# Pair weights applied at the copy out of PSUM, and the last layernorm stage handed out again among the engines

## Chip, cores and metric

One core of a Trainium2 chip runs the kernel. The metric is the device time of one execution in microseconds (us). TensorE is named PE in the profile, VectorE DVE, ScalarE ACT, GpSimd POOL and SyncE SP; PEld is PE's loading of weights.

## The reference

For x of 8 batches x 512 tokens x 128 channels (all f32):

```
x = x + layernorm(attn(layernorm(x)))          # a decaying scan between two 128x128 products
h = layernorm(x)
logits = h @ gate                              # 8 experts
w, e = top_k(logits, 2);  w = softmax(w)
out_k = (silu(h @ w0[e_k]) * (h @ w1[e_k])) @ wo[e_k]      # 128 -> 512 -> 128, k = 0, 1
x = x + layernorm(w_0 * out_0 + w_1 * out_1)
```

The softmax over two logits depends on their gap only: with gap = second logit - first logit and t = tanh(gap / 2), the first weight is 0.5 - 0.5 t and the second 0.5 + 0.5 t.

## The kernel before

**Attention part.** It works batch by batch (four tiles of 128 tokens each) and ends, per batch, with the normalised rows `row` (128 channels, then a column with the token's number and a column with its first expert), the two chosen experts, and for each (token, choice) a place in the DRAM tensor `expert_rows`, where every expert has a region. POOL writes them there with 8 indirect DMAs a batch (`send_row`, L394). `top` (L808 to L820) also keeps the gap of the two best logits in `logit_gap`.

**Expert part.** There are 71 tiles (`TILES`) of up to 128 rows of one expert. The code of every engine runs through the same `slots()`: slot t holds x transposed for tile t, the two first layers of tile t-1, the transposing of the gated values of t-2, the last layer of t-3 and the copying out and sending of t-4. SP loads each tile's rows (`load_tile`, L312) into a ring `taken_rows` of 16. ACT does `first_part` (L570, x rounded to x_hi), `take_y` (L587, the last layer's result from PSUM to `y_rows`, a plain copy), `gate_curve` (L575, silu) and `gated_turned` (L580). DVE does `rest_part` (L1099, x_lo), `times_gate_curve` (L1106) and, once in four tiles (`PAIRS`), `pairs_of_tiles` (L1118, L1122), which finds for four tiles whether a row is its token's second choice (`not_first`) and where its result goes (`y_pair`). POOL sends a tile's y with one indirect DMA to `pair_rows` (`send_y`, L405). While batches remain, each phase of 8 slots also carries parts of the attention work (`a_slot`), between the tiles' own instructions; the first 48 tiles (`FULL_TILES`) lie in such phases. `OLD_TILES` is 63: from there on tiles hold only rows of the last batch.

**Last stage.** `pair_rows` holds 2 x 128 values for each token. SP waits until the y of the first 63 tiles has landed and reads batches back in five groups (`GROUPS`: batch 0; 1 and 2; 3 and 4; 5 and 6; 7), the last group after all 71 (L343). A group then goes through:

- DVE `sum_pairs` (L1146): out_0 + r * out_1 with r = w_1 / w_0, one scalar_tensor_tensor per tile of tokens;
- DVE `stats_of` (L1154) and `aggregate` (L1160), then `scaled` (L1165), the variance times w_0 squared;
- POOL `one_over_sd`: plus eps (L438), to the power -0.5 (L442);
- DVE `scale` (L1171), times w_0, and `offset` (L1176);
- ACT `normalise4` (L593), one activation per tile of tokens;
- POOL (L465), in the last group DVE (L1284), adds the result to x; SP writes x to `out` (L351).

`weights` makes w_0, w_0 squared and r once, in slot 61, from ACT's tanh of all gaps (L643, slot 59). The order on DVE is written out by a loop over groups (L1268): sums and statistics of group g stand before scale and offset of group g-1. Group 0's sum lies in slot 69, its statistics in slot 70, its `one_over_sd` on POOL in slot 71, and its `normalise4` on ACT in slot 73, ahead of the last tile's `take_y` in slot 74. After the slots POOL does, for g = 0 to 3, `one_over_sd(g + 1)` and then group g's add, one instruction per group.

Of the kernel before, what the change touches and what calls it, by code (L numbers as in the profile page):

```python
# [14 lines left out]
P = 128  # L15
# [7 lines left out]
ROW = D + 2  # L23
# [27 lines left out]
W_SPLITS = 8  # L51
GROUPS = ((0, 1), (1, 3), (3, 5), (5, 7), (7, 8))


def sandwich_kernel(nc, x_in, w_in_in, b_in_in, w_out_in, b_out_in, decay_in, mix_in,
                    gate_in, w0_in, w1_in, wo_in, out):
    ctx = ExitStack()
    with ctx:
# [70 lines left out]
        logit_gap = sb("logit_gap", [P, B * G])  # L129
        weight = sb("weight", [P, K, B * G])  # L130
        denom = sb("denom", [P, B * G])
        half1 = sb("half1", [P, B * G])
        weight0_square = sb("weight0_square", [P, B * G])
# [25 lines left out]
        not_first = sb("not_first", [P, PAIRS])  # L159
        y_pair = pair("y_pair", [P, PAIRS], I32)  # L160
# [18 lines left out]
        def pair_tile(n, k):  # L179
            at = (n % G * K + k) * D  # L180
            return pairs_in[n // G][:, at:at + D]
# [3 lines left out]
        scaled_var, sd4, inv4, rs4, nm4 = (sb(n, [P, B * G]) for n in (  # L185
            "scaled_var", "sd4", "inv4", "rs4", "nm4"))
# [14 lines left out]
        def before_in(bank_of, b):  # L201
# [13 lines left out]
                   "xn2T_ps xn2T gate_ps gap top8 choice choice_f onehot taken total "  # L215
# [7 lines left out]
        names_c = "xeT_ps x_hi x_lo l1_ps l2_ps silu gated gatedT_ps gatedT y_ps y not_first y_pair"  # L223
# [4 lines left out]
        names_d = "out_end m stats mv scaled sd inv rs nm normed out x1"  # L228
        d = {n: sem("d_" + n) for n in names_d.split()}
        s_exp, s_weight = sem("exp"), sem("weight")  # L230
# [31 lines left out]
        def sums(n):  # L262
            return pair_tile(n, 0)

        def normed_of(first, end):

            return pairs_of(first, end).rearrange("p (n k d) -> p n k d", k=K, d=D)[:, :, 0, :]
# [15 lines left out]
        def _(sp):  # L283
# [73 lines left out]
        def _(pool):  # L357
# [78 lines left out]
            def one_over_sd(g, first, end):  # L436
                pool.wait_ge(d["scaled"], g + 1)
                pool.tensor_tensor(  # L438
                    sd4[:, first * G:end * G], scaled_var[:, first * G:end * G],
# [3 lines left out]
                    inv4[:, first * G:end * G], sd4[:, first * G:end * G],  # L443
                    minus_half[:].broadcast_to([P, (end - first) * G]),
                    ALU.pow).then_inc(d["inv"], 1)
# [16 lines left out]
            for g, (first, end) in enumerate(GROUPS[:-1]):  # L462
# [6 lines left out]
        def _(act):  # L469
# [168 lines left out]
            for k, s, t in slots():  # L638
# [6 lines left out]
                elif t == TILES + 2:  # L645
                    normalise4(0, *GROUPS[0])
# [846 lines left out]
```

## Time and profile before

| | us |
|---|---|
| median of 3 runs | 347.58 (345.55 to 349.6) |
| the profiled execution | 350.95 |
| its span, first to last instruction | 349.2 |
| mean granted TensorE clock | 0.858 of 2.4 GHz |

Busy shares of the span: PE 75%, DVE 57%, POOL 52%, ACT 51%. All rows are of the profiled execution, whose own time is 1.75 us above its span. Times of rows are counted from the span's start. The duration in a row is that of the instruction or the merged group; "[idle before <-releaser]" is the time its engine had stood idle and what ended it.

### The profile page before, as it was taken

Reading aid. Unit: us, or ns where it says so; the run is one execution under the profiler, and the core shown is the slowest. Engines: PE = TensorE matmul, PEld = TensorE weight load, DVE = VectorE, ACT = ScalarE, POOL = GpSimd, SP = SyncE. Lnnn points to the kernel's source line nnn. Section 1 sums busy time; section 2 is a strip of 40 time slices with the busy share of each in tenths; the row PEclk is TensorE's granted clock in tenths of the full one; section 3 lists DMA queues with packets and bytes.
Section 4 is the critical chain, followed back from the end, with each engine's and each line's share of the span. In section 5 each row is a group of like instructions: output and inputs, shape, how many; then the busy total and the mean of one; then the engine's idle time right before and its main releaser. Section 6 shows DMA issues by size and latency. Waiting matters only on the chain.

```text
span 349.2 us, 6768 instructions
## 1 busy us (share of the span) xinstructions
PE 262.5 (75%) x1615; PEld 220.8 (63%) x1615; DVE 199.7 (57%) x896; ACT 179.4 (51%) x436; POOL 180.1 (52%) x199
## 2 busy tenths in 40 slices
PE   1645515579997999699969969969999999995000
PEld 0323513468785888588858858848888888885000
DVE  4787969564662495348347625633334455459763
ACT  3475635345654566354545544524655565554362
POOL 6065567155465656545754764465333333335673
PEclk9975555589999899789989998998999999999555
DMA  6999111211221131013112211331233100190225
GB/s 160 225 362 281 41 38 55 52 33 41 60 57 46 41 76 48 30 52 81 41 35 64 57 47 42 83 92 55 69 85 79 42 23 23 31 401 29 90 60 150
DMA packets 27971, 29.48 MB, mean 84 GB/s; under 512 B 4538, under 2 KB 21148, under 8 KB 27936
## 3 DMA queue, kind: packets, MB, share of 16 engines
q1 hardware_dynamic: 22672, 20.00, 20.2%
q0 software_dynamic: 4544, 8.93, 8.0%
q8 instruction: 16, 0.26, 0.3%
q10 hardware_dynamic: 720, 0.13, 0.2%
q14 instruction: 19, 0.16, 0.2%
HBM read 17.49 MB, written 12.01 MB: 84 GB/s over the span
## 4 chain that ended last, share of the span: by engine, by line
PE 60%; DVE 15%; ACT 8%; another core or an unknown queue 6%; POOL 4%; issue 4%; DMA 2%; SPq 0%; ACTq 0%; DVEq 0%; POOLq 0%
PE bank L1432 14%; PE bank L1381 9%; PE bank L1383 9%; PE bank L1382 8%; PE bank L1416 8%; PE bank L1376 3%; POOL expert_rows L394 2%; PE bank L1317 2%; PE bank L1333 2%; ACT sb_w_raw L593 2%; DVE sb_rs L1171 2%; PE bank L1326 2%; ACT sb_row L524 1%; PE bank L1306 1%
## 5 line engine op out<-in xcount | busy, mean ns | idle before, releaser
L405 POOL DMA_INDIRECT pair_rows<-sb_y_rows,sb_y_pair x71 | 70.4, 991 | 99.3 <-ACT sb_y_rows L587 75.2
L394 POOL DMA_INDIRECT expert_rows<-sb_row,sb_place x64 | 65.1, 1016 | 32.0 <-issue 18.0
L1106 DVE TENSOR_TENSOR sb_w_raw<-bank,sb_w_raw 128x512 f32<-128x512 f32 x71 | 49.0, 690 | 51.9 <-PE bank L1383 33.7
L1432 PE MATMUL bank<-sb_w_raw,sb_gatedT 128*128 x568 | 76.4, 279 | 0.0
L1432 PEld LDWEIGHTS bank<-sb_w_raw,sb_gatedT 128*128 128x128 f32 x568 | 70.6, 196 | 0.1
L1381 PE MATMUL bank<-sb_w_parts,sb_x_hi 128*128 x142 | 65.2, 459 | 3.5 <-ACT sb_w_raw L575 1.9
L580 ACT ACTIVATE sb_gatedT<-bank 128x512 f32<-128x512 f32 x71 | 42.5, 599 | 45.3 <-PE bank L1416 32.0
L1099 DVE TENSOR_TENSOR sb_x_lo<-bank,sb_x_hi 128x128 fp32r<-128x128 f32 x71 | 20.4, 288 | 66.9 <-ACT sb_x_hi L570 60.6
L1383 PE MATMUL bank<-sb_w_parts,sb_x_hi 128*128 x142 | 58.5, 412 | 0.0
L1382 PE MATMUL bank<-sb_w_parts,sb_x_lo 128*128 x142 | 58.1, 409 | 0.0
L575 ACT ACTIVATE sb_w_raw<-bank 128x512 f32<-128x512 f32 x71 | 42.7, 601 | 18.4 <-PE bank L1383 14.3
L570 ACT ACTIVATE sb_x_hi<-bank 128x128 fp32r<-128x128 f32 x71 | 19.7, 277 | 58.2 <-PE bank L1376 35.7
L1416 PE MATMUL bank<-sb_ident,sb_w_raw 128*128 128x128 f32 x284 | 44.2, 280 | 0.4 <-issue 0.4
L1416 PEld LDWEIGHTS bank<-sb_ident,sb_w_raw 128*128 128x128 f32 x284 | 35.5, 144 | 9.9 <-issue 2.6
L1381 PEld LDWEIGHTS bank<-sb_w_parts,sb_x_hi 128*128 128x128 f32 x142 | 28.2, 199 | 10.3 <-issue 6.9
L1383 PEld LDWEIGHTS bank<-sb_w_parts,sb_x_hi 128*128 128x128 f32 x142 | 28.1, 198 | 7.0
L1382 PEld LDWEIGHTS bank<-sb_w_parts,sb_x_lo 128*128 128x128 f32 x142 | 28.4, 200 | 3.2
L1376 PE MATMUL bank<-sb_ident,sb_taken_rows 128*128 128x128 f32 x71 | 20.4, 287 | 4.6 <-DMA sb_taken_rows<-expert_rows 4.0
L587 ACT ACTIVATE sb_y_rows<-bank 128x128 f32<-128x128 f32 x71 | 19.5, 274 | 1.0 <-PE bank L1432 0.9
L1306 PE MATMUL bank<-sb_early,sb_w_inT 128*128 128x512 f32 x16 | 11.4, 803 | 10.2 <-DVE sb_early L757 10.2
L1326 PE MATMUL bank<-sb_ident,sb_row 128*128 128x128 f32 x32 | 7.5, 378 | 14.4 <-ACT sb_row L524 14.3
L256 POOL TENSOR_TENSOR sb_w_parts<-sb_w_raw,sb_w_parts 128x512 fp32r<-128x512 f32 x8 | 9.9, 1271 | 15.4 <-ACT sb_w_parts L537 15.4
(162 smaller groups left out, 353.4 us busy)
## 6 DMA issues: line engine op xcount, KB each, us to landing
sb_taken_rows<-expert_rows SPq DMA_DIRECT2D x71, 65.0 KB
sb_w_raw<-in_L_ffn_w SPq DMA_DIRECT2D x2, 2048.0 KB, 15.1
sb_w_raw<-pair_rows SPq DMA_DIRECT2D x2, 1024.0 KB, 7.8
out_dram<-sb_x SPq DMA_DIRECT2D x3, 512.0 KB, 3.2
pair_rows<-sb_y_rows,sb_y_pair POOLq DMA_INDIRECT x71
sb_x<-in_L_attn_x SPq DMA_DIRECT2D x4, 256.0 KB, 5.5
expert_rows<-sb_row,sb_place POOLq DMA_INDIRECT x64
sb_w_raw<-pair_rows SPq DMA_DIRECT2D x2, 512.0 KB, 3.4
```

Source lines behind the costliest of these rows:

```text
L394: pool.indirect_dma_start(expert_rows[:, :], bass.IndirectOffsetOnAxis(ap=place[b % ROWS][:, k, j:j + 1], axis=0), row[b % ROWS][:, j, :], ...
L405: pool.indirect_dma_start(pair_rows[:, :], bass.IndirectOffsetOnAxis(ap=y_pair[group % 2][:, t % PAIRS:t % PAIRS + 1], axis=0), y_rows[slo ...
L575: act.activation(silu[t % 2][:], p_l1[:], ACT.Silu).then_inc(c["silu"], 1)
L580: act.activation(gatedT[t % 2][:], p_gatedT[:], ACT.Copy).then_inc(c["gatedT"], 1)
L1099: dve.tensor_tensor(x_lo[t % 2][:], p_xeT[:, 0:P], x_hi[t % 2][:].bitcast(F32), ALU.subtract).then_inc(c["x_lo"], 1)
L1106: dve.tensor_tensor(gated[t % 2][:], p_l2[:], silu[t % 2][:], ALU.mult).then_inc(c["gated"], 1)
L1376: pe.transpose(p_xeT[:, 0:P], taken_rows[:, t % RING, 0:D], ident[:]).then_inc(c["xeT_ps"], 1)
L1381: pe.matmul(to, x_hi, w_hi, start=True, stop=False)
L1382: pe.matmul(to, x_lo, w_hi, start=False, stop=False)
L1383: return pe.matmul(to, x_hi, w_lo, start=False, stop=True)
L1416: last = pe.transpose(p_gatedT[:, n * P:(n + 1) * P], gated[t % 2][:, n * P:(n + 1) * P], ident[:])
L1432: last = pe.matmul(p_y[t % 2][:, 0:D], gatedT[t % 2][:, n * P:(n + 1) * P], wo.rearrange("p o d -> p (o d)"), start=(n == 0), stop=(n == F ...
```

## The change

- `expert_rows` and `taken_rows` get a further column (rows of 131 values instead of 130) that holds the token's gap. It is written in `top` in place of `logit_gap`.
- Once in four tiles ACT takes tanh(gap / 2) of these columns (`tanh_of_gaps`, after `take_y` in the slot), and DVE makes the weight from it with two small instructions at the end of `pairs_of_tiles`: `signed` = (not_first - 0.5) * tanh, `y_weight` = signed + 0.5. `take_y` scales the copy by it, a [128, 1] operand in SBUF, and waits for it at the first tile of each four.
- `weights`, `scaled` and `scale` go away. `sum_pairs` is one tensor_tensor add of 512 columns per batch.
- All steps of the last stage go by batch instead of by group, only 1/sd and the offset by group. Batch 0's sum moves to slot 68, its statistics to 69, its 1/sd on POOL to 70; slot 70 also holds the sums of batches 1 and 2, slot 71 the statistics of batch 1 and the offset of group 0. `normalise4` of batch 0 moves on ACT from slot 73 to behind all slots.
- DVE takes over `normalise4` of batch 6 (tensor_scalar per tile) and the adds of batches 5, 6 and 7, the last in two halves. POOL adds batches 0 to 4, one instruction each.

```diff
-ROW = D + 2
+ROW = D + 3
+HERE, NORMED_HERE = 5, 6
...
@@ SP
-                if g < len(GROUPS) - 1:
-                    sp.wait_ge(d["out"], g + 1)
+                if end <= HERE:
+                    sp.wait_ge(d["out"], end)
                 else:
-                    sp.wait_ge(d["out_end"], 1)
+                    sp.wait_ge(d["out_end"], end - HERE)
...
@@ POOL
+            def add_normed(b):
+                pool.wait_ge(d["normed"], b + 1)
+                pool.tensor_tensor(x[:, b * G:(b + 1) * G], x[:, b * G:(b + 1) * G],
+                                   half_of_pairs(b, 0), ALU.add).then_inc(d["out"], 1)
...
-                if t == OLD_TILES + 8:
+                if t == OLD_TILES + 7:
                     one_over_sd(0, *GROUPS[0])
...
+            one_over_sd(1, *GROUPS[1])
+            add_normed(0)
+            one_over_sd(2, *GROUPS[2])
+            add_normed(1)
+            add_normed(2)
+            one_over_sd(3, *GROUPS[3])
+            add_normed(3)
+            one_over_sd(4, *GROUPS[4])
+            add_normed(4)
@@ ACT
-                    act.activation(y_rows[t % Y_SLOTS][:], p_y[t % 2][:, 0:D],
-                                   ACT.Copy).then_inc(c["y"], 1)
+                    group = t // PAIRS
+                    if t % PAIRS == 0:
+                        wait_apart(act, c["y_weight"], group + 1)
+                    act.activation(y_rows[t % Y_SLOTS][:], p_y[t % 2][:, 0:D], ACT.Copy,
+                                   scale=y_weight[group % 2][:, t % PAIRS:t % PAIRS + 1]
+                                   ).then_inc(c["y"], 1)
+            def tanh_of_gaps(t):
+                if not is_tile(t) or (t % PAIRS != PAIRS - 1 and t != TILES - 1):
+                    return
+                first, group = t - t % PAIRS, t // PAIRS
+                n, ring = t + 1 - first, first % RING
+                act.activation(tanh_gap[group % 2][:, 0:n], taken_rows[:, ring:ring + n, D + 2],
+                               ACT.Tanh, scale=0.5).then_inc(c["tanh"], 1)
...
             for g, (first, end) in enumerate(GROUPS):
-                if g:
-                    normalise4(g, first, end)
+                for b in range(first, end):
+                    if b != NORMED_HERE:
+                        normalise4(g, b)
@@ DVE
-                dve.tensor_tensor(logit_gap[:, b * G:(b + 1) * G], top8[n][:, :, 1],
-                                  top8[n][:, :, 0], ALU.subtract).then_inc(a["gap"], 1)
+                dve.tensor_tensor(row[b % ROWS][:, :, D + 2], top8[n][:, :, 1],
+                                  top8[n][:, :, 0], ALU.subtract)
...
+                dve.wait_ge(c["tanh"], group + 1)
+                dve.scalar_tensor_tensor(
+                    out=signed[:, 0:n], in0=not_first[:, 0:n], scalar=-0.5,
+                    in1=tanh_gap[group % 2][:, 0:n], op0=ALU.add,
+                    op1=ALU.mult).then_inc(c["signed"], 1)
+                dve.wait_ge(c["signed"], group + 1)
+                dve.tensor_scalar(y_weight[group % 2][:, 0:n], signed[:, 0:n], 0.5, None,
+                                  ALU.add).then_inc(c["y_weight"], 1)
...
+                dve.tensor_tensor(half_of_pairs(b, 0), half_of_pairs(b, 0), half_of_pairs(b, 1),
+                                  ALU.add).then_inc(d["m"], 1)
...
+            def normalise4(g, b):
+                dve.wait_ge(d["nm"], g + 1)
+                for n in range(b * G, (b + 1) * G):
+                    last = dve.tensor_scalar(sums(n), sums(n), rs4[:, n:n + 1], nm4[:, n:n + 1],
+                                             ALU.mult, ALU.add)
+                last.then_inc(d["normed_here"], 1)
...
+            def add_last():
+                for j in range(0, G, 2):
+                    dve.wait_ge(d["normed_end"], j + 2)
+                    last = dve.tensor_tensor(
+                        x[:, (B - 1) * G + j:(B - 1) * G + j + 2],
+                        x[:, (B - 1) * G + j:(B - 1) * G + j + 2],
+                        half_of_pairs(B - 1, 0)[:, j:j + 2], ALU.add)
+                last.then_inc(d["out_end"], 1)
...
+                if t == OLD_TILES + 5:
+                    sum_pairs(0, 0)
                 elif t == OLD_TILES + 6:
+                    stats_of(0)
+                    aggregate(0)
                 elif t == OLD_TILES + 7:
+                    sum_pairs(1, 1)
+                    sum_pairs(1, 2)
+                elif t == OLD_TILES + 8:
+                    stats_of(1)
+                    offset(0)
...
+            stats_of(2)
+            aggregate(1)
+            aggregate(2)
+            sum_pairs(2, 3)
+            sum_pairs(2, 4)
+            stats_of(3)
+            stats_of(4)
+            offset(1)
+            aggregate(3)
+            aggregate(4)
+            sum_pairs(3, 5)
+            sum_pairs(3, 6)
+            stats_of(5)
+            stats_of(6)
+            offset(2)
+            aggregate(5)
+            aggregate(6)
+            sum_pairs(4, 7)
+            stats_of(7)
+            offset(3)
+            aggregate(7)
+            normalise4(3, 6)
+            offset(4)
+            add_normed(5)
+            add_normed(6)
+            add_last()
```

## Rows read from the trace of the kernel before

**Rows 1.** Stretch, length, busy us of PE, PEld, DVE, ACT, POOL; clock; DMA share.
```profile
250.00:311.00 61.00, 61.00 (x412) 54.27 (x412) 28.25 (x68) 35.49 (x87) 21.61 (x22) 1.00 0.27 80
...
320.00:349.20 29.20, 0.00 (x0) 0.00 (x0) 18.66 (x84) 12.89 (x33) 16.48 (x14) 0.53 0.29 90
```

**Rows 2.** Timeline of one tile slot: start, duration, engine, line, [idle before, releaser].
```profile
303.67 1.32 SPq L343 DMA_DIRECT2D sb_w_raw<-pair_rows  x3
...
305.21 0.17 DVE L1122 TENSOR_TENSOR sb_y_pair<-sb_not_first,sb_taken_rows 128x4 int32<-128x4 f32 x1
...
305.96 0.27 ACT L587 ACTIVATE sb_y_rows<-bank 128x128 f32<-128x128 f32 x1
...
306.48 0.60 ACT L575 ACTIVATE sb_w_raw<-bank 128x512 f32<-128x512 f32 x1 [0.25 <-PE bank L1383]
```

**Rows 3.** Timeline, the last tiles and the start of the last stage.
```profile
315.64 0.69 DVE L1106 TENSOR_TENSOR sb_w_raw<-bank,sb_w_raw 128x512 f32<-128x512 f32 x1 [0.37 <-ACT sb_w_raw L575]
...
317.22 2.10 PE L1432 MATMUL bank<-sb_w_raw,sb_gatedT 128*128 x16
...
319.44 0.98 POOL L405 DMA_INDIRECT pair_rows<-sb_y_rows,sb_y_pair  x1 [0.35 <-issue]
...
323.53 0.98 POOL L405 DMA_INDIRECT pair_rows<-sb_y_rows,sb_y_pair  x1 [3.11 <-ACT sb_y_rows L587]
...
324.82 1.67 POOL L442 TENSOR_TENSOR sb_inv<-sb_sd,sb_minus_half 128x8 f32<-128x8 f32 x1
...
326.47 1.25 POOL L465 TENSOR_TENSOR sb_x<-sb_x,sb_w_raw 128x512 f32<-128x512 f32 x1
326.52 1.23 DVE L1171 TENSOR_TENSOR sb_rs<-sb_inv,sb_weight 128x8 f32<-128x8 f32 x1 [1.76 <-POOL sb_inv L442]
```

**Rows 4.** Timeline, the rest of the last stage.
```profile
334.68 1.13 DVE L1146 SCALAR_TENSOR_TENSOR sb_w_raw<-sb_w_raw,sb_weight 128x128 f32<-128x128 f32 x4
...
335.16 1.65 POOL L442 TENSOR_TENSOR sb_inv<-sb_sd,sb_minus_half 128x8 f32<-128x8 f32 x1
335.85 0.87 DVE L1154 BATCH_NORM_STATS2 sb_stats<-sb_w_raw 128x6 f32<-128x128 f32 x4
...
336.93 0.37 DVE L1160 BATCH_NORM_AGGREGATE sb_mv<-sb_stats 128x2 f32<-128x6 f32 x4
...
340.21 0.20 POOL L438 TENSOR_TENSOR sb_sd<-sb_scaled_var,sb_eps 128x4 f32<-128x4 f32 x1
...
341.54 2.30 DVE L1171 TENSOR_TENSOR sb_rs<-sb_inv,sb_weight 128x4 f32<-128x4 f32 x1 [4.04 <-POOL sb_inv L442]
...
344.07 1.65 ACT L593 ACTIVATE sb_w_raw<-sb_w_raw,sb_nm,sb_rs 128x128 f32<-128x128 f32 x4 [3.16 <-DVE sb_nm L1176]
345.74 0.69 DVE L1284 TENSOR_TENSOR sb_x<-sb_x,sb_w_raw 128x512 f32<-128x512 f32 x1 [1.71 <-ACT sb_w_raw L593]
```

**Rows 5.** Groups by line and form: count, busy us, mean ns, idle before.
```profile
L508 ACT ACTIVATE sb_early<-bank,sb_one_minus_mix 128x511 f32<-128x511 f32 x8 | 5.5, 689 | 2.7 <-PE bank L1298 2.7
...
L791 DVE TENSOR_TENSOR sb_x<-sb_x,sb_nm 128x512 f32<-128x512 f32 x8 | 5.4, 680 | 0.0
...
L633 ACT ACT_TABLE_LOAD x1 | 1.3, 1283 | 0.0
...
L643 ACT ACTIVATE sb_weight<-sb_logit_gap 128x32 f32<-128x32 f32 x1 | 0.2, 232 | 0.0
```

**Rows 6.** Chain that ended last, in the phases: start us, us, what.
```profile
107.74 4.42 another core or an unknown queue
...
143.92 0.27 ACT sb_y_rows L587
...
202.68 2.74 another core or an unknown queue
```

**Rows 7.** The page's DMA issues: count, KB each, us to landing.
```profile
out_dram<-sb_x SPq DMA_DIRECT2D x3, 512.0 KB, 3.2
...
sb_w_raw<-pair_rows SPq DMA_DIRECT2D x2, 512.0 KB, 3.4
```

More of the change, by code:

```diff
@@ L221, in sandwich_kernel @@
         s_b, s_table = sem("table_step"), sem("table")
-        names_c = "xeT_ps x_hi x_lo l1_ps l2_ps silu gated gatedT_ps gatedT y_ps y not_first y_pair"
+        names_c = ("xeT_ps x_hi x_lo l1_ps l2_ps silu gated gatedT_ps gatedT y_ps y not_first y_pair "
+                   "tanh signed y_weight")
         c = {n: sem("c_" + n) for n in names_c.split()}
@@ L458, in _ @@
                 a_slot(k, s)
-                if t == OLD_TILES + 8:
+                if t == OLD_TILES + 7:
                     one_over_sd(0, *GROUPS[0])
-            for g, (first, end) in enumerate(GROUPS[:-1]):
-                one_over_sd(g + 1, *GROUPS[g + 1])
-                pool.wait_ge(d["normed"], g + 1)
-                pool.tensor_tensor(x[:, first * G:end * G], x[:, first * G:end * G],
-                                   normed_of(first, end), ALU.add).then_inc(d["out"], 1)
+            one_over_sd(1, *GROUPS[1])
[7 more added lines that the diff above has]
+            add_normed(4)
         @block.scalar
@@ L640, in _ @@
                 take_y(t - 4)
-                if t == OLD_TILES - 4:
-                    act.wait_ge(a["gap"], B)
-                    act.activation(weight[:, 1, :], logit_gap[:], ACT.Tanh,
-                                   scale=0.5).then_inc(s_exp, 1)
-                elif t == TILES + 2:
-                    normalise4(0, *GROUPS[0])
+                tanh_of_gaps(t)
                 a_slot(k, s, 0)
@@ L1143, in sum_pairs @@
-            def sum_pairs(g, first, end):
-                dve.wait_ge(s_pairs_in[g], 16)
-                for n in range(first * G, end * G):
-                    last = dve.scalar_tensor_tensor(
-                        out=sums(n), in0=pair_tile(n, 1),
-                        scalar=weight[:, 1, n:n + 1], in1=sums(n), op0=ALU.mult, op1=ALU.add)
-                last.then_inc(d["m"], 1)
-            def stats_of(g, first, end):
-                dve.wait_ge(d["m"], g + 1)
-                for n in range(first * G, end * G):
+                dve.wait_ge(c["tanh"], group + 1)
@@ L1154, in stats_of, with aggregate @@
+            def stats_of(b):
+                dve.wait_ge(d["m"], b + 1)
+                for n in range(b * G, (b + 1) * G):
                     last = dve.bn_stats(stats4[:, n, :], sums(n))
                 last.then_inc(d["stats"], 1)
-            def aggregate(g, first, end):
-                dve.wait_ge(d["stats"], g + 1)
-                for n in range(first * G, end * G):
+            def aggregate(b):
+                dve.wait_ge(d["stats"], b + 1)
+                for n in range(b * G, (b + 1) * G):
@@ L1174, in offset @@
-            def offset(g, first, end):
+            def offset(g):
+                first, end = GROUPS[g]
                 dve.wait_ge(d["rs"], g + 1)
```

96 lines of the change are left out of this document (26 added, 70 removed).

## The prediction

> **What bounds the kernel now.** I read the busy times by stretch first, then the timeline of one tile slot, then the timeline and the chain of waits of the last stage. From 250 to 311 us PE is busy all of the 61 us, at the full granted clock of 2.4 GHz, and DVE, ACT and POOL stand at 28, 35 and 22 us [rows 1]: the tile slots of 2.84 us belong to PE. After 320 us PE has nothing to do. The 29.2 us that follow are the last stage, in which DVE is busy 18.7 us, POOL 16.5 and ACT 12.9 [rows 1]: no engine is full, they wait for one another.
>
> Two things make these waits. First, POOL's send of the last tile's y starts at 323.53, after 3.11 us of idling for ACT's copy [rows 3]: ACT had to finish `normalise4` of group 0 before that copy, though PE was done with the tile at 317.22 + 2.10 = 319.32. Behind the send stand eps and power of group 1, which end at 324.82 + 1.67 = 326.49. Second, POOL's add to x holds up DVE: at 326.47 it starts for 1.25 us, and `scale`, 8 columns, started at 326.52, takes 1.23 us and ends with it [rows 3]. At 341.54 the same kind of instruction takes 2.30 us beside a two-batch add, and only then can ACT normalise the last group, 1.65 us from 344.07, and DVE add it, until 345.74 + 0.69 = 346.43 [rows 4]. Writing out takes the span to 349.2.
>
> **Tile slots.** ACT's copy of y gets a [128, 1] scale. A copy from PSUM with such a scale takes 689 ns for 511 columns [rows 5], silu without it 0.60 us for 512 [rows 2]: 0.09 us more, so 0.36 for a y. Silu stood idle 0.25 us waiting for PE [rows 2], which covers that; the tanh, once in four tiles, costs at most the 232 ns of L643 [rows 5] and less where it overlaps its neighbours, so together about the 0.25. DVE's gated product waits for PE's second layer anyway. The two new DVE instructions follow y_pair, started at 305.21 for 0.17 [rows 2], at about 0.17 us each with a wait between: y_weight is there at about 305.75, y is copied at 305.96 at the earliest. I take 0 here, since PE is full; if nothing covered it, the price would be 71 x 0.09 = 6.4 us (the other bound; below). A change of activation table does not come: the only load for this part stands at L633, and tanh at L643 ran between silus with none [rows 5]. `weights` goes out of slot 61, which was covered too: 0. The 131st column adds 0.8% to the rows' bytes: 0.
>
> In the phases the chain does pass ACT. There are four stretches in which PE's completions reach nobody, the first 4.42 us at 107.74, the last 2.74 at 202.68, and behind one y stands in the chain with its 0.27 [rows 6]. I charge 0.09 in each of six phases and round to +0.6 us. Below zero there is nothing to find, as no instruction leaves that chain.
>
> **Last stage.** Steps, from rows: a 512-column add on DVE 0.68 (L791, rows 5), about 0.65 in a row; statistics of a batch 0.87, 1.64 for two; aggregates 0.37, 0.64 for two (rows 4 for the single ones); offset 0.15; on POOL eps and power of a two-batch group 326.49 - 324.51 = 1.98, of one batch 341.5 - 340.21 = 1.3, an add of one batch 1.25 [rows 3, 4]. Batch 0's sum in slot 68 needs its load: issued 303.67 [rows 2], plus 3.4 us [rows 7] is 307.1; the gated product, through just before y_pair's two instructions at 305.0 in slot 67 [rows 2], is through at 307.85 in slot 68. So slots 68 to 71 run without a stall, and what DVE has there is about as long as before. From 316.3 (end of the last product, rows 3) DVE has statistics, two offsets' worth, aggregates and sums up to batch 4, 5.4 us, and is at `offset` of group 1 at 321.7.
>
> *Send.* With `normalise4` of batch 0 behind the slots, ACT copies the last y at 319.32 to 319.7. POOL is busy with the send before until 319.44 + 0.98 = 320.42, where 0.35 us lay between sends [rows 3]: 320.7 to 321.7. Eps and power end at 323.7 instead of 326.49. The last group's load moves up alike: it is asked for some 2.25 us after the last send starts (an estimate: SP issued it 2.25 us after 323.53) and lands 3.4 us later, 326.4.
>
> *Round 1.* POOL's add of batch 0 starts at 323.7 before DVE's offset, as at 326.47, and holds it: offset 1 is out at 325.1. *Round 2.* Aggregates of 3 and 4: 325.7; POOL 1.98: 327.7, then add 1 to 328.95. DVE meanwhile does sums and statistics of 5 and 6, until 328.65; offset 2 is out at 329.2. *Round 3.* POOL's add 2 ends at 330.4 (DVE's sum of 7 waits for it, statistics at 331.9), eps and power of group 3 at 332.4, add 3 at 333.65 with offset 3 held: 333.8. *Round 4.* Aggregate of 7: 334.15; DVE then normalises batch 6, four instructions at some 0.2 (bounds: 0.15, the smallest ones, and 0.28, as statistics over the same 128 columns), beside POOL's 1.3 us: 335.5. Add 4 ends at 336.75, offset 4 at 336.9. *End.* ACT takes 1.65 for batch 7, until 338.6; DVE's adds of 5 and 6 fit in that; the second half of the last add, some 0.42 us, ends at 339.1, against 346.43: 7.3 us earlier.
>
> *Writing out.* Before, 2.77 us passed from 346.43 to the end. Now batches 5 and 6 (512 KB, 3.2 us to landing [rows 7]) are issued at 338.3 and batch 7 just behind: 0.4 us more. The last stage thus gives 6.9 us.
>
> **A rule against it.** POOL's add held DVE's `scale` for its whole time [rows 3, 4]. The Trainium skill (SBUF — State Buffer, Who interferes with whom) says that a DVE instruction with two inputs in SBUF, or a `tensor_scalar` in a two-port mode, and a GpSimd instruction that reads SBUF exclude each other for the whole instruction. The trace agrees for the adds (1.23 and 2.30 us), but not for the power: the four sums at 334.68 take 1.13 beside the power at 335.16, as long as alone [rows 4]. By the rule as it stands sums 5 and 6 and the new normalising on DVE would wait behind powers or hold them; by the row they don't, and the sum goes by the row.
>
> **Sum.** 6.9 - 0.6 = 6.3 us. Span 349.2 - 6.3 = 342.9, the profiled execution's own time 350.95 - 6.3 = 344.65. That execution was slower than the median of the runs, 347.58; off the median it makes 341.3 us, 1.8% less. A change of about 1% is what a measurement of this kernel can tell from none (the runs lie between 345.55 and 349.6), so 344.1 and 351.1 are the borders.
>
> **Rivals.** (A) POOL's adds don't hold the offsets, since they are other instructions (scalar_tensor_tensor) than the held ones, or get the port first. For it: none of them was seen beside an add. Against: the held one also had two SBUF inputs. Then offset 1 is out at 323.85, rounds 3 and 4 come 2.8 us earlier: 338.5.
> (B) The power and eps do exclude DVE's adds and its normalising. Round 2 gets one power's wait of about 1 us, round 4 some 0.8: 343. Against it stand the sums of rows 4.
> (C) The copy of y is not covered: ACT hands over later, POOL and the next slot follow. 71 x 0.09 = 6.4 us, the 0.6 among it: 341.3 + 5.8 = 347.1, no change. Against it: PE full at 61.00 of 61.00 [rows 1].
> (D) Slower. The silent stretches of PE (four, 4.42 to 2.74 us, rows 6) all follow the slot with s = 3, the end of a group of four tiles, where ACT and DVE now get three more instructions. The same comes at s = 7 as well. A further one costs about 3.8 us, and some 2 us more at 1.2 GHz behind it. One more leaves a gain of 0.5; from the second on the kernel is slower: 341.3 + 2 x 5.8 = 352.9. Against it: from slot 48 on group ends brought none.
>
> **Chances.** The forecast 0.50, A 0.15, B 0.15, C 0.13, D 0.07. Faster by over 1%: forecast 0.47, A 0.15, B 0.12, C 0.03 (half of it covered), together 0.77. Within 1%: 0.03 + 0.03 + 0.10 = 0.16. Slower: D, 0.07. The range of 337.0 to 345.5 takes in A, the forecast and B, with 1.5 us around for the silent stretches' lengths, and leaves out most of C and D.
>
> **What would show it.** The y copies at 0.36 us and slots from 48 on still 2.84 us apart; POOL's last send at about 4.4 us after the last gated product's end, not 7.2; offsets of groups 1, 3 and 4 taking over 1 us each beside an add; from the last matmul's end to the last DVE add 19.8 us where it was 27.1. It is wrong if the slots are longer than 2.84, if silent stretches grow in number, or if DVE's sums or its normalising show durations over 1 us beside a power.

## The result, and the profile after

| | before | after |
|---|---|---|
| median (14 runs each) | 348.58 us (345.55 to 351.2) | 344.43 us (343.2 to 345.86) |
| ratio, with its 95% interval | | 0.9898 (0.9869 to 0.9927) |
| the profiled execution, its span | 350.95, 349.2 | 344.83, 343.1 |
| mean granted clock | 0.858 | 0.878 |

The change makes the kernel 1.0% faster; 1.8% was forecast. Ratios are formed over fast runs alone (those within 1.5% of the fastest run of their kernel), so they are not the quotient of the medians, which is 0.9881 here. Two more comparisons of the same two kernels, below, give 1.8% and 1.4%. The interval of the second (0.9775 to 0.9868) just misses that of the first, so sessions differ by a little more than the intervals say.

A span falls into two parts at one instant, the end of PE's last matmul (the start of its row plus 2.10 us). Before it stands everything with tiles; behind it only the last stage. Two stretches of the changed kernel answer to [rows 1]. Columns: stretch, length, busy us of PE, PEld, DVE, ACT, POOL, clock, DMA share, GB/s.

```profile
250.00:311.00 61.00, 61.00 (x412) 54.24 (x411) 29.78 (x77) 37.56 (x92) 21.61 (x22) 1.00 0.27 83
318.70:343.10 24.40, 0.00 (x0) 0.00 (x0) 15.94 (x56) 11.56 (x29) 16.04 (x15) 0.54 0.37 108
```

PE is still full in the tile slots, and from 250 to 311 it executes the same 412 matmuls as before: DVE's 1.5 us and ACT's 2.1 us of additional work lie beside it. The last stage takes 24.4 us. Before it took 349.2 - 319.32 = 29.9. So 5.5 of the 6.1 us between the two spans come from the last stage, and 0.6 from where the last matmul ends (319.32 and 318.70). That instant moves by several us between executions of one kernel, as the experiments show, so the 0.6 says nothing of the tile part.

**The tile slot.** Rows of one slot of the changed kernel, from its timeline:

```profile
302.74 0.21 ACT L605 ACTIVATE sb_tanh_gap<-sb_taken_rows 128x4 f32<-128x4 f32 x1
...
304.58 0.17 DVE L1139 TENSOR_TENSOR sb_y_pair<-sb_not_first,sb_taken_rows 128x4 int32<-128x4 f32 x1
304.67 0.15 DVE L1144 SCALAR_TENSOR_TENSOR sb_signed<-sb_not_first,sb_tanh_gap 128x4 f32<-128x4 f32 x1
304.85 0.17 DVE L1149 TENSOR_SCALAR sb_y_weight<-sb_signed 128x4 f32<-128x4 f32 x1
...
305.33 0.37 ACT L594 ACTIVATE sb_y_rows<-bank,sb_y_weight 128x128 f32<-128x128 f32 x1
...
305.85 0.60 ACT L579 ACTIVATE sb_w_raw<-bank 128x512 f32<-128x512 f32 x1 [0.15 <-PE bank L1414]
```

The weight is out at 305.02, the copy of y starts at 305.33 and takes 0.37 us where it took 0.27 [rows 2], and silu's idle time shrinks from 0.25 to 0.15: the cover named in the prediction, seen at work. Over all tiles the groups of the changed kernel give the same (count, busy us, mean ns, idle before):

```profile
L594 ACT ACTIVATE sb_y_rows<-bank,sb_y_weight 128x128 f32<-128x128 f32 x71 | 25.9, 365 | 2.0 <-PE bank L1463 1.6 <-issue 0.4
```

**The last stage.** Timeline of the changed kernel from the last matmul on; POOL's sends are L400, eps L433, power L437, adds L444; DVE's offset is L1172, its sums L1154.

```profile
316.60 2.10 PE L1463 MATMUL bank<-sb_w_raw,sb_gatedT 128*128 x16
...
320.21 0.98 POOL L400 DMA_INDIRECT pair_rows<-sb_y_rows,sb_y_pair  x1 [0.30 <-issue]
321.20 0.23 POOL L433 TENSOR_TENSOR sb_sd<-sb_mv,sb_eps 128x8 f32<-128x8 f32 x1
321.51 1.67 POOL L437 TENSOR_TENSOR sb_rs<-sb_sd,sb_minus_half 128x8 f32<-128x8 f32 x1
...
323.16 1.25 POOL L444 TENSOR_TENSOR sb_x<-sb_x,sb_w_raw 128x512 f32<-128x512 f32 x1
323.21 1.23 DVE L1172 SCALAR_TENSOR_TENSOR sb_nm<-sb_mv,sb_rs 128x8 f32<-128x8 f32 x1 [2.60 <-POOL sb_rs L437]
...
324.91 1.26 DVE L1154 TENSOR_TENSOR sb_early<-sb_early 128x512 f32<-128x512 f32 x2
325.07 0.56 POOL L433 TENSOR_TENSOR sb_sd<-sb_mv,sb_eps 128x8 f32<-128x8 f32 x1 [0.66 <-DVE sb_mv L1166]
325.71 1.97 POOL L437 TENSOR_TENSOR sb_rs<-sb_sd,sb_minus_half 128x8 f32<-128x8 f32 x1
...
332.43 1.26 POOL L444 TENSOR_TENSOR sb_x<-sb_x,sb_w_raw 128x512 f32<-128x512 f32 x1
332.50 1.22 DVE L1172 SCALAR_TENSOR_TENSOR sb_nm<-sb_mv,sb_rs 128x8 f32<-128x8 f32 x1 [0.92 <-POOL sb_rs L437]
...
333.93 1.08 DVE L1180 TENSOR_SCALAR sb_early<-sb_early,sb_rs,sb_nm 128x128 f32<-128x128 f32 x4
...
335.37 1.26 POOL L444 TENSOR_TENSOR sb_x<-sb_x,sb_w_raw 128x512 f32<-128x512 f32 x1
335.43 1.22 DVE L1172 SCALAR_TENSOR_TENSOR sb_nm<-sb_mv,sb_rs 128x4 f32<-128x4 f32 x1 [0.42 <-POOL sb_rs L437]
336.57 1.28 DVE L1189 TENSOR_TENSOR sb_x<-sb_x,sb_early 128x512 f32<-128x512 f32 x2
...
338.36 0.43 DVE L1195 TENSOR_TENSOR sb_x<-sb_x,sb_w_raw 128x256 f32<-128x256 f32 x1 [0.18 <-ACT sb_w_raw L611]
```

The last send follows its predecessor by 0.30 us instead of idling 3.11 [rows 3]. Each offset beside an add takes 1.22 to 1.23 us, as `scale` did. The last DVE add ends at 338.79, 20.1 us behind the last matmul's end; before it was 27.1. Then 4.3 us pass to the end of the span, where it was 2.8 [rows 4]. The stretch of the last writes:

```profile
337.50:342.20 4.70, 0.00 (x0) 0.00 (x0) 1.11 (x3) 0.83 (x3) 0.00 (x0) 0.50 0.97 278
```

The DMA engines are busy 97% of these 4.7 us, at 278 GB/s: 1280 KB, batches 3 to 7, go out without a gap. [rows 7] had 3.2 us from issue to landing for 512 KB, with nothing else being written.

### The profile page after: what moved, and what is told of

The parts are those of the page before. It is cut to its first block, busy times and chain, and to the rows that moved or that the text cites. A ratio compares the mean times of both kernels' runs of the same rounds, so it can differ in the third digit from the quotient of the medians.

```text
span 343.1 us, 6803 instructions
## 1 busy us (share of the span) xinstructions
PE 262.9 (77%) x1615; PEld 219.6 (64%) x1615; DVE 200.1 (58%) x900; ACT 185.8 (54%) x449; POOL 179.3 (52%) x200
## 4 chain that ended last, share of the span: by engine, by line
PE 61%; DVE 10%; ACT 8%; another core or an unknown queue 7%; POOL 6%; issue 4%; DMA 2%; POOLq 0%; SPq 0%; ACTq 0%; DVEq 0%
PE bank L1463 14%; PE bank L1412 9%; PE bank L1447 9%; PE bank L1414 8%; PE bank L1413 8%; PE bank L1407 3%; PE bank L1348 2%; POOL expert_rows L389 2%; PE bank L1357 2%; POOL sb_rs L437 2%; PE bank L1364 1%; ACT sb_row L528 1%; PE bank L1337 1%; ACT sb_w_raw L579 1%
## 5 line engine op out<-in xcount | busy, mean ns | idle before, releaser
L400 POOL DMA_INDIRECT pair_rows<-sb_y_rows,sb_y_pair x71 | 70.4, 992 | 97.1 <-ACT sb_y_rows L594 80.2
L1463 PE MATMUL bank<-sb_w_raw,sb_gatedT 128*128 x568 | 75.5, 276 | 0.0
L1463 PEld LDWEIGHTS bank<-sb_w_raw,sb_gatedT 128*128 128x128 f32 x568 | 69.6, 193 | 0.1
L1116 DVE TENSOR_TENSOR sb_x_lo<-bank,sb_x_hi 128x128 fp32r<-128x128 f32 x71 | 20.4, 288 | 64.0 <-ACT sb_x_hi L574 62.0
L574 ACT ACTIVATE sb_x_hi<-bank 128x128 fp32r<-128x128 f32 x71 | 19.7, 278 | 53.3 <-PE bank L1407 33.7
L594 ACT ACTIVATE sb_y_rows<-bank,sb_y_weight 128x128 f32<-128x128 f32 x71 | 25.9, 365 | 2.0 <-PE bank L1463 1.6
L1407 PE MATMUL bank<-sb_ident,sb_taken_rows 128*128 128x128 f32 x71 | 20.4, 288 | 5.4 <-DMA sb_taken_rows<-expert_rows 4.0
L1337 PE MATMUL bank<-sb_early,sb_w_inT 128*128 128x512 f32 x16 | 12.2, 856 | 9.9 <-DVE sb_early L774 9.9
```

The lines of the kernel that those rows point to most:

```text
L400: pool.indirect_dma_start(pair_rows[:, :], bass.IndirectOffsetOnAxis(ap=y_pair[group % 2][:, t % PAIRS:t % PAIRS + 1], axis=0), y_rows[slo ...
L594: act.activation(y_rows[t % Y_SLOTS][:], p_y[t % 2][:, 0:D], ACT.Copy, scale=y_weight[group % 2][:, t % PAIRS:t % PAIRS + 1]).then_inc(c[" ...
L1407: pe.transpose(p_xeT[:, 0:P], taken_rows[:, t % RING, 0:D], ident[:]).then_inc(c["xeT_ps"], 1)
L1463: last = pe.matmul(p_y[t % 2][:, 0:D], gatedT[t % 2][:, n * P:(n + 1) * P], wo.rearrange("p o d -> p (o d)"), start=(n == 0), stop=(n == F ...
```

## The experiments

All ratios are against the kernel before, run in the same session; it stands at 353.61 us beside e0 to e3, 354.47 beside e4 to e7 and the second e1, 349.61 beside f0 to f2 and e8, 353.54 beside g1 to g4, 353.88 beside h1 and h2, so medians of different sessions are not compared. "Last stage" is the time from the last matmul's end to the end of the span, "last add" from there to DVE's last add.

| run | median us (runs) | ratio (95%) | last matmul ends | last stage | last add |
|---|---|---|---|---|---|
| e0_after | 346.29 (6) | 0.9821 (0.9775 to 0.9868) | 319.6 | 24.4 | 20.1 |
| e1_tail_only | 349.25 (6) | 0.9857 (0.9817 to 0.9897) | 325.3 | 24.3 | 20.1 |
| e2_tiles_only | 355.43 (12) | 1.0068 (1.0030 to 1.0107) | 323.0 | 29.9 | |
| e3_adds_wait | 347.19 (6) | 0.9807 (0.9768 to 0.9846) | 324.2 | 24.9 | 19.7 |
| e4_write_each | 347.71 (1) | | 322.6 | 23.4 | 20.1 |
| e6_add4_first | 349.74 (1) | | 325.1 | 22.9 | 19.8 |
| e7_adds_dve | 345.03 (4) | 0.9713 (0.9621 to 0.9804) | 324.2 | 20.4 | 16.7 |
| e1_tail_only_2 | 348.58 (1) | | 322.5 | 24.3 | |
| f0_after | 344.52 (6) | 0.9860 (0.9802 to 0.9918) | 317.8 | 24.3 | |
| f1_tail_only | 345.37 (6) | 0.9868 (0.9795 to 0.9940) | 315.3 | 24.4 | |
| f2_tiles_only | 352.01 (12) | 1.0087 (1.0045 to 1.0130) | 319.8 | 29.9 | |
| e8_rows_spread | 339.33 (6) | 0.9738 (0.9682 to 0.9793) | 313.3 | 24.3 | |
| g1_row131 | 354.99 (12) | 1.0042 (1.0001 to 1.0083) | 322.5 | 29.9 | |
| g2_best | 340.38 (6) | 0.9636 (0.9590 to 0.9683) | 319.5 | 20.4 | |
| g3_before_spread | 351.26 (12) | 0.9934 (0.9898 to 0.9971) | 320.7 | 29.8 | |
| g4_tiles_spread | 352.22 (12) | 0.9973 (0.9941 to 1.0005) | 319.9 | 30.0 | |
| h1_no_write_56 | 343.85 (1) | | 318.8 | 23.3 | 20.1 |
| h2_no_write_34 | 345.70 (1) | | 320.2 | 23.7 | 20.1 |

e1, e2, f1, f2, g4, h1 and h2 leave out work or do some twice, so that their output is another one; they serve to price a part.

One thing stands out: the last stage repeats to 0.1 us or so wherever its code is the same, while the instant before it moves from 313 to 325 us, and for one and the same kernel (e1, its repeat, f1) from 315.3 to 325.3. A single profile settles a question about the last stage, and none about the tiles.

### The two halves of the change

e0_after and f0_after are the changed kernel as it is.

> The changed kernel itself, as the mark for the others of this call. Theory 1 (the last stage gives about 5.5 us and the tile part takes some of it back): about 4 us below the kernel before, and again some 24.4 us from the last matmul's end to the end of the span, 29.9 before. Theory 2 (the 14 runs of before were high by chance): 5.5 to 6 us below. The write of the results again runs without a gap for about 4.5 us at the end.

> The changed kernel beside the two that follow, again on one chip. The stretch from the last matmul's end to the end gives 5.5 us against before on any chip. Theory 2 (what lies before the last matmul does not differ between before and after but by chance: it starts at 64 to 67 us and has phases of 31 or 33 us): 1.6% below before, 1.2 to 2.0. Theory 1 (the tile part costs some 1.3 us): 1.2% below, 0.9 to 1.5.

e1_tail_only (with its repeats) keeps the new last stage and the 131 columns, and leaves the weights of y out, so the output lacks them:

```diff
-                act.activation(y_rows[...], p_y[...], ACT.Copy, scale=y_weight[...])
+                act.activation(y_rows[...], p_y[...], ACT.Copy)
-                tanh_of_gaps(t)
-                dve.scalar_tensor_tensor(out=signed ...)
-                dve.tensor_scalar(y_weight ...)
```

> Leaves out the weights: y is copied plain, no tanh, no weights from it; the last stage is that of the changed kernel (the output is the unweighted sum). Theory 1 (the tile part costs about 1.3 us in the phases, where y stands in the chain with 0.09 us more and DVE's two instructions more): 1.0 to 1.5 us faster than the changed kernel. My prediction said 0.6. Theory 2 (the tile part is covered everywhere): within 0.3 us of it. Rival C of the prediction (the copy is not covered): 6 us faster.

> e1_tail_only again, for its trace: phases of 8 tiles last 31 or 33 us by whether the clock stays at 1.2 GHz for 3.4 or 6.8 us behind a silent stretch. If that is chance, the long phases fall elsewhere than in the first run (phases 2, 4) and the last matmul's end moves by 1 to 4 us; if the kernel fixes it, they fall alike. Slots 48 to 70 again last 62.4 us.

> The last stage of the change without the weights at the copy, again. Theory 1: 1 to 1.5 us faster than f0_after. Theory 2: within 1 us of it either way; together with the first measurement (3 us slower there) no sign that the tile part costs anything in the phases. In slots 48 to 70 (62.4 us) the tile part is worth at most 0.1 us.

e2_tiles_only is the kernel before with the new tile part (131 columns, tanh, weights, scaled copy) on top; its old last stage still weights, so the weights enter twice:

```diff
-ROW = D + 2
+ROW = D + 3
...
+                tanh_of_gaps(t)
...
+                act.activation(y_rows[...], p_y[...], ACT.Copy, scale=y_weight[...])
```

> The kernel before with the tile part of the change alone: 131 columns, tanh and weights once in four tiles, y scaled; its last stage is unchanged and weights a second time, so the output is another one. Theory 1: 1.0 to 1.5 us slower than before. Theory 2: no difference. Rival C: 6 us slower.

> The tile part alone on the kernel before, again. Theory 1: 1 to 1.5 us slower than before. Theory 2: within 1 us of before.

The two sessions of the changed kernel don't decide between the theories: e0 gained 7.3 us in the medians, more than either said (about 4, and 5.5 to 6), and the 1.4% of f0 lies within both. The repeat e1_tail_only_2 has its long phases at the same places as e1 (the second and the fourth), but they last 32.0 and 32.1 us instead of 33.1 and 33.0, and its last matmul ends 2.8 us earlier.

Measured: the last stage alone is worth 5.5 to 5.6 us in every trace. The tile part, on the old kernel, costs 0.7% and 0.9% in two sessions: 2.4 and 3.0 us, of which the intervals leave 1.1 to 4.5. Taken away from the changed kernel, all but the wider rows (e1 against e0, f1 against f0), it gives nothing back: the ratios rise by 0.4 and 0.1 points, inside their intervals. So the whole tile part has a price on the old kernel, and what was taken away on the new one (tanh, weights, scaled copy) shows none; the wider rows stayed there, and nothing prices them on the new kernel. The trace says why it can't be read as so much per slot. From tile 48 to tile 70 the first activations of the tiles lie 62.2 us apart before, 62.5 after and 62.4 in e2: at most 0.3 us for 22 slots. The rest is left to what comes before tile 48, where the silent stretches lie. It was not found in a row there, since the phases differ by a us between two traces of one kernel (33.1 us in e1, 32.0 for the same phase of its repeat).

g1_row131 is the kernel before with 131 columns, the last holding the gap, which nobody reads:

```diff
-ROW = D + 2
+ROW = D + 3
...
+                dve.tensor_tensor(row[b % ROWS][:, :, D + 2], top8[n][:, :, 1],
+                                  top8[n][:, :, 0], ALU.subtract)
```

> The kernel before with rows of 131 values, the gap written into the new column and not used (one small DVE instruction per batch more). If the width of the rows is what made e2_tiles_only and f2_tiles_only 2.4 to 2.7 us slower than before, this is 2 to 3 us slower too, and the silent stretches grow. If the cost is the scaled copy, the tanh and the weights, it is within 0.7 us of before.

It costs 0.4%, with zero just outside the interval. The wider rows may therefore be half of the tile part's price; with an interval of 0.01% to 0.83% no more is to be said.

### What holds the offsets

e3_adds_wait lets POOL's adds of batches 0, 1, 3 and 4 wait until DVE's offset is out:

```diff
-            def add_normed(b):
+            def add_normed(b, offsets=0):
+                wait(pool, d["nm"], offsets)
                 pool.wait_ge(d["normed"], b + 1)
```

> The changed kernel with one wait more in front of POOL's adds: each waits until DVE's offset that becomes ready at the same moment is out. If POOL's add holds DVE's offset for its whole time (1.23 us each, four times in the trace of after, three with POOL's add starting 50 ns ahead), the offsets take 0.15 us each, and the last DVE add ends 2.5 to 3.5 us earlier; the span falls by as much, less what the writing takes back (about 0.5). If the long offsets are something else, such as waits for an operand, nothing moves.

Its timeline, DVE's and POOL's rows around the first add and the normalising of batch 6:

```profile
328.66 0.17 DVE L1173 SCALAR_TENSOR_TENSOR sb_nm<-sb_mv,sb_rs 128x8 f32<-128x8 f32 x1 [2.60 <-POOL sb_rs L437]
...
329.30 2.03 DVE L1155 TENSOR_TENSOR sb_early<-sb_early 128x512 f32<-128x512 f32 x2
...
338.34 1.99 DVE L1181 TENSOR_SCALAR sb_early<-sb_early,sb_rs,sb_nm 128x128 f32<-128x128 f32 x4
...
340.84 2.36 DVE L1190 TENSOR_TENSOR sb_x<-sb_x,sb_early 128x512 f32<-128x512 f32 x2
```

```profile
328.91 1.27 POOL L445 TENSOR_TENSOR sb_x<-sb_x,sb_w_raw 128x512 f32<-128x512 f32 x1 [0.28 <-DVE sb_nm L1173]
...
338.21 1.26 POOL L445 TENSOR_TENSOR sb_x<-sb_x,sb_w_raw 128x512 f32<-128x512 f32 x1 [0.28 <-DVE sb_nm L1173]
...
341.01 1.65 POOL L445 TENSOR_TENSOR sb_x<-sb_x,sb_w_raw 128x512 f32<-128x512 f32 x1 [0.28 <-DVE sb_nm L1173]
```

The offsets take 0.17 us instead of 1.23, so it was the adds that held them. But the last add comes only 0.4 us earlier (19.7 for 20.1) where 2.5 to 3.5 were expected, and the last stage takes 0.5 us more (24.9 for 24.4): the sums take 2.03 instead of 1.26, the normalising 1.99 instead of 1.08, DVE's adds 2.36 instead of 1.28. The hold goes on to the next DVE instructions.

e7_adds_dve takes the adds off POOL altogether; DVE does all eight, and each batch is written by itself:

```diff
-            add_normed(0)      # POOL, and 1 to 4
...
+            add_normed(0)      # DVE, behind stats_of(6); 1 and 2 behind aggregate(6);
+            add_normed(3)      # behind aggregate(7); 4 behind offset(4)
```

> All adds to x on DVE, in its order where their inputs are ready; POOL keeps eps and power; each batch is written at once. If POOL's adds cost DVE their own length wherever they stand (the wait moved from the offsets to the sums in e3_adds_wait), five adds of 1.25 us on POOL are dearer than five of 0.65 us on DVE: the last DVE add comes at 17.5 to 18 us behind the last matmul's end instead of 20.1, the end at 20.5 to 21.5 instead of 24.4, and the kernel is 2.5 to 4 us faster than the changed one. If DVE's own work is the limit, the five adds put 3.2 us on its path and the last add comes at 20 or later.

```profile
328.75 0.17 DVE L1160 SCALAR_TENSOR_TENSOR sb_nm<-sb_mv,sb_rs 128x8 f32<-128x8 f32 x1 [2.60 <-POOL sb_rs L437]
...
332.13 0.67 DVE L1177 TENSOR_TENSOR sb_x<-sb_x,sb_w_raw 128x512 f32<-128x512 f32 x1
...
340.22 0.76 DVE L1184 TENSOR_TENSOR sb_x<-sb_x,sb_w_raw 128x256 f32<-128x256 f32 x2
```

An add is 0.67 us on DVE and 1.25 on POOL, where it costs DVE 0.8 to 1.1 us of waiting besides. Without it the last add comes 16.7 us behind the last matmul and the last stage takes 20.4 us: 4.0 less than in the changed kernel, 3.0 less than in e4, which has the same eight writes.

### What sets the end

e4_write_each writes each batch by itself instead of in five groups:

```diff
-            for g, (first, end) in enumerate(GROUPS):
+            for first, end in [(n, n + 1) for n in range(B)]:
```

> The changed kernel, but SP writes each batch as soon as it is added (8 writes of 256 KB instead of 5 by group). In the changed kernel the last three writes, 1280 KB, run without a gap for 4.5 us (284 KB/us) and begin 0.9 us after the add of batch 4. If the writes set the end, batch 3 is out of the way 2.5 us earlier, 1024 KB remain, and the stretch from the last matmul's end to the end falls from 24.4 to about 23.5 us with the last DVE add where it was (20.1). If the DVE add sets the end, it stays at 24.4.

e6_add4_first is e4 with POOL's add of batch 4 ahead of the last group's 1/sd:

```diff
-            one_over_sd(4, *GROUPS[4])
             add_normed(4)
+            one_over_sd(4, *GROUPS[4])
```

> As e4_write_each, and POOL adds batch 4 before it makes 1/sd of batch 7 instead of behind it. If the writes set the end: batch 4's write starts 1.7 us earlier, 768 KB remain, and the stretch falls to about 22.4 us. The last DVE add comes 0 to 0.3 us earlier, since the last offset is no longer held by the add, but waits 1.2 us longer for the power. If only the offsets' release sets the end, 24.1 to 24.4.

h1_no_write_56 and h2_no_write_34 are the changed kernel without one write, so 512 KB of the output are missing:

```diff
             for g, (first, end) in enumerate(GROUPS):
+                if g == 3:       # h2: g == 2
+                    continue
```

> The changed kernel without its write of batches 5 and 6 (512 KB of out are left out; all else as it is). Read is the time from the last matmul's end to the end of the span, 24.4 us with all writes. Backlog theory: the last three writes, 1280 KB, run without a gap at 284 KB per us, so the end is set by the bytes that become ready late. Without 512 KB the write of 3 and 4 is through 1.8 us after it starts (337.6 in the trace, so 339.4), batch 7 starts about 1.0 us after the last add's end at 338.79 and takes 0.9: the bytes end at 340.7 instead of 342.2, and the tail is 22.9. Fixed-cost theory (a write takes so long from its issue, whatever else is under way): 24.4, unchanged. Last add at 20.1 us in both.

> The changed kernel without its write of batches 3 and 4 (512 KB of out left out; all else as it is). Backlog theory: batches 5 and 6 start about 1.0 us after their adds' end at 337.85 and are followed by batch 7 without a gap: 768 KB by 284 is 2.7 us, until 341.6 instead of 342.2, tail 23.8. If what was written before did not matter: 24.4. If the write of 3 and 4 were the whole of the lateness: 22.9 or less.

The last stage takes 24.4 us as it is, 23.4 when batch 3 need not wait for batch 4 (e4), 22.9 when batch 4 is ready earlier as well (e6), 23.7 without batches 3 and 4, 23.3 without 5 and 6. The last add lies at 20.1 in all of them but e6 (19.8), so what moves is only the time from there to the end: 4.3, 3.4, 3.1, 3.6 and 3.2 us. Windows of the traces of h1 and then of h2:

```profile
337.50:339.50 2.00, 0.00 (x0) 0.00 (x0) 1.25 (x3) 0.96 (x3) 0.00 (x0) 0.50 0.90 257
339.50:341.00 1.50, 0.00 (x0) 0.00 (x0) 0.00 (x0) 0.00 (x0) 0.00 (x0) 0.50 0.64 182
```

```profile
340.20:343.10 2.90, 0.00 (x0) 0.00 (x0) 0.08 (x1) 0.00 (x0) 0.00 (x0) 0.50 0.92 271
```

In h1 the queue runs dry for a moment (share 0.64) before batch 7, and its end is the time of batch 7 alone. h2 keeps the queue full with 768 KB that all became ready late. The backlog forecast 22.9 and 23.8 and measured are 23.3 and 23.7; a fixed cost per write would have left 24.4 twice. For e6 it forecast 22.4, and measured is 22.9. So the bytes that wait at the end set it, to within half a us.

### Where the sends of rows stand

e8_rows_spread is the changed kernel with POOL's eight row sends of a phase distributed 2, 1, 1, 1, 1, 2 over its slots 0 to 5, where it was 1, 1, 2, 1, 2, 1:

```diff
                 if s == 0:
                     send_row(sent, 0)
+                    send_row(sent, 1)
...
                 elif s == 2:
-                    send_row(sent, 2)
                     send_row(sent, 3)
...
                 elif s == 5:
+                    send_row(sent, 6)
                     send_row(sent, 7)
```

> The changed kernel with the 8 row sends of a batch spread otherwise over the slots (2, 1, 1, 1, 1, 2 for s = 0 to 5 in place of 1, 1, 2, 1, 2, 1). If the silent stretches behind slot s = 3 come from POOL's four sends in a row there, they get shorter by 1 us or more each (3.8 us in the changed kernel) or move to s = 0 or s = 5, and the kernel is 3 to 5 us faster or the phases change their length. If POOL's sends have nothing to do with them, they stay at s = 4 with 3.7 to 4.5 us.

It is 1.2 points faster than f0_after beside it (5.2 us in the medians), and the two intervals don't overlap; the last stage is unchanged. Two of its phases, then the same two of f0_after, the changed kernel in the same session (columns as above):

```profile
95.60:125.20 29.60, 27.81 (x186) 23.06 (x185) 17.38 (x87) 17.60 (x46) 18.81 (x20) 1.00 0.20 55
125.20:155.00 29.80, 27.85 (x186) 23.14 (x186) 17.53 (x88) 17.61 (x47) 18.82 (x20) 1.00 0.20 56
```

```profile
93.90:124.76 30.86, 27.39 (x186) 23.29 (x185) 17.42 (x87) 17.80 (x46) 18.80 (x20) 1.00 0.19 54
124.76:156.96 32.20, 28.84 (x186) 24.33 (x185) 17.65 (x87) 18.18 (x46) 18.81 (x20) 0.95 0.19 53
```

PE has the same 186 matmuls in each. In the first phase the granted clock is 1.00 (2.4 GHz) in both kernels, and yet e8 is 1.3 us shorter: PE stands idle 1.8 us of it instead of 3.5, and is busy 0.4 us more. In the second the clock is 1.00 instead of 0.95, which is 1.0 us of busy time, and the idle time 1.9 instead of 3.4. Over the four phases from 93.9 us in f0_after (124.6 us) and from 95.6 in e8 (118.8), PE is busy 1.8 us less and idle 4.0 us less. The chain of f0_after and that of e8 show what lies ahead:

```profile
106.53 3.76 another core or an unknown queue
137.28 4.49 another core or an unknown queue
169.53 3.71 another core or an unknown queue
```

```profile
99.73 3.13 another core or an unknown queue
109.87 0.92 another core or an unknown queue
129.40 3.09 another core or an unknown queue
136.82 2.09 another core or an unknown queue
```

The silence of a phase is not shorter in e8 (3.13 + 0.92 us against 3.76, 3.09 + 2.09 against 4.49); it is cut in two pieces. PE works on through the first part of a silence and stands idle for the rest, and that rest is what shrinks. Where PE starts again in the first phase of the changed kernel, of f0_after and (two rows) of e8:

```profile
112.55 1.12 PE L1357 MATMUL bank<-sb_ident,sb_row 128*128 128x128 f32 x4 [3.05 <-ACT sb_row L528]
```

```profile
112.36 0.66 PE L1357 MATMUL bank<-sb_ident,sb_row 128*128 128x128 f32 x4 [3.11 <-ACT sb_row L528]
```

```profile
103.63 0.63 PE L1447 MATMUL bank<-sb_ident,sb_w_raw 128*128 128x128 f32 x4 [0.55 <-ACT sb_gatedT L584]
112.85 0.66 PE L1357 MATMUL bank<-sb_ident,sb_row 128*128 128x128 f32 x4 [0.87 <-ACT sb_row L528]
```

The clock does not follow from the length of such an idle time alone: behind the 3.05 us of the changed kernel it was at 1.2 GHz (0.50 from 113 to 115 us), behind the 3.11 us of f0_after at 2.4 (1.00 from 112 to 117 us), and the same four matmuls take 1.12 us and 0.66. What is won is mostly idle time of PE, and in some phases the clock on top.

Three further kernels: the kernel before with this spread (g3), e2 with it (g4), and e7 with it (g2).

> The kernel before with the row sends spread alone. If POOL's sends in a row make the silent stretches whatever else the kernel does, its phases come to 29.7 us as in e8_rows_spread and it is 3 to 6 us faster than before, with the last stage at 29.9 us.

> e2_tiles_only with the row sends spread. With phases of even length the price of the tile part should show without the chance of 31 or 33 us. If ACT's and DVE's added instructions stand in the chain themselves, it is 1 us or more slower than g3_before_spread. If what e2_tiles_only lost came from longer silent stretches alone, it is within 0.6 us of g3_before_spread.

> The changed kernel with e7_adds_dve (all adds on DVE, writes by batch) and e8_rows_spread (row sends 2, 1, 1, 1, 1, 2). If both gains stand for themselves (4.0 us of the last stage, 5.2 of the phases): 335 to 337 us where the changed kernel takes 344 to 346, 3.5 to 4% below before; from the last matmul's end to the end 20.4 us, phases of 29.7 us.

The spread gives the kernel before only 0.7% (2.3 us, where 3 to 6 were expected): its silences are cut in two as well, but its phases last 30.7 to 32.2 us, and the clock holds at 1.00 in two of the four and is 0.95 in the others. With the tile part (g4) it is 1.00 in all four and they last 30.3 to 30.6 us, yet the time is 0.4 points above g3's; the intervals overlap, so the price of the tile part stays open here. g2 puts both gains together: 3.6% below the kernel before, against 1.0 to 1.8% for the change. Its phases last 29.9 to 30.3 us and, at a clock of 0.95, 31.1 in the fourth; 29.7 was expected.

## Why the prediction was right or wrong

**What bounds it, and the direction: right.** PE full in the slots, the last stage a chain of waits, and the gain there.

**Tile slots: right from tile 48 on, too low in the phases of the old kernel.** The copy of y took 365 ns where 360 were said, tanh 0.21, the two DVE instructions 0.15 and 0.17, all covered. But "I charge 0.09 in each of six phases" gave 0.6 us, and e2 and f2 show 2.4 and 3.0 on the old kernel; "The 131st column adds 0.8% to the rows' bytes: 0" may be part of it (g1, 0.4%, just above nothing). With the new last stage no price of tanh, weights and scaled copy shows (e1, f1); there the wider rows were not priced.

**The chain of the last stage: right to 0.3 us at its end, 0.4 to 0.7 us late in between.** Counted from the last matmul's end, the last send ended at 2.5 us (forecast 321.7 - 319.32 = 2.4), offset 1 was out at 5.7 (5.8), the second power ended at 9.0 (8.4), the third at 13.8 (13.1), offset 4 was out at 18.0 (17.6), the last add ended at 20.1 (19.8).

**The step that failed: writing out.** "Now batches 5 and 6 (512 KB, 3.2 us to landing [rows 7]) are issued at 338.3 and batch 7 just behind: 0.4 us more" took the duration of one write on an empty queue [rows 7]. It was 1.5 us more: 4.3 us from the last add to the end instead of 2.8. It left out that batches 3 and 4 would still be on their way. Batches 3 and 4 become ready at 336.6, 5 and 6 at 337.9 and 7 at 338.8, three writes within 2.2 us that need 4.6 us of a full queue; e4, e6, h1 and h2 move the end by moving or removing those bytes alone. So the last stage gave 5.5 us where 6.9 were said, 1.1 of the difference by the writing and 0.3 by the chain.

**The rest of the sum.** With 5.5 - 0.6 = 4.9 us the gain would have been 1.4%, which is the middle of the three comparisons (1.0, 1.8, 1.4%). That it meets the middle is no proof of the 0.6: with the 2.4 to 3.0 us of e2 and f2 in its place the gain would be 2.5 to 3.1 us (0.7 to 0.9%), just below the lowest of the three. The first comparison gave 4.15 us in the medians; the 0.75 missing there is left to what lies before the last matmul, which differs by several us between traces of the same last stage, and was not traced to an instruction. The 344.43 lies in the stated range (337.0 to 345.5), though the sum promised 2.1 us more than came. The 347.58 that the forecast started from, a median of three runs, was itself 1.0 us below that of 14.

**Rivals.** A is excluded: the adds do hold the offsets, and neither order tried on POOL (e3, e6) moved the last add by more than 0.4 us. B is half true. The Trainium skill's rule (SBUF — State Buffer, Who interferes with whom) speaks of exclusion for the whole instruction; the trace agrees where DVE's 512-column sums came first (eps 0.56 instead of 0.23, power 1.97 instead of 1.67 us) and not where four `tensor_scalar` lay beside a power of 4 columns (1.08 and 1.02 us, both undisturbed), though an add on POOL did hold the same four (1.99 in e3). The second power ended 0.6 us later than said, the last add 0.3. C is excluded by the windows. D did not come in time, but its sign did in part. The chain of the kernel before has six silent pieces, one of them at 231.77 for 3.71 us, which the prediction's "four" passed over; that of the changed kernel has nine. In the phases up to 219 us they stand at the same places, the first two of 3.8 instead of 4.4 us; the sixth phase has five instead of one, of 1.6 to 2.7 us, and is no longer for it (28.7 us, before 29.3). e8 shows that their place and length depend on where POOL's sends stand.

## What to carry to other kernels

Sum the bytes that become ready in the last microseconds, and divide by the rate of a full queue; the latency of one write on an empty queue is not their price. Here a 512-column GpSimd add of 1.25 us beside VectorE's work on SBUF cost 0.8 to 1.1 us of VectorE's time as well; where the end hangs on VectorE, moving the add there can be cheaper than ordering around it (20.4 us against 23.4, and against 22.9 with another order, the writes alike). And where profiles of the same part repeat to 0.1 us while the rest moves by several, compare that part alone, and the whole only over many runs.

## What was not expected of the hardware

- The hold is passed on. Delaying POOL's add by 0.28 us behind DVE's offset freed the offset (0.17 us) and lengthened the next DVE instructions by 0.8 to 1.1 us instead; DVE's `tensor_scalar` with two operands per partition is held as well (1.99 and, in e6, 1.84 us for four, 1.08 with no add beside them).
- In each phase there are stretches of 2 to 4.5 us in which no completion of PE reaches another engine. Cut in two by other places of POOL's sends, they cost PE less idle time: 1.8 and 1.9 us instead of 3.5 and 3.4 in the two phases shown, which are 1.3 and 2.4 us shorter. The granted clock then stays at 1.00 in all four phases of e8 and g4, but not of g3 and g2. What makes the silence itself stays open: that it moves with POOL's sends is shown, how is not.
- The last matmul of the changed kernel ends at 319.6, 317.8 and 318.7 us in three profiles from three sessions, and that of e1's kernel at 325.3, 322.5 and 315.3, with the same work before it.
